# Attention on one core: scores in plain rotation of three banks, maxima handled two by two

## The reference

```
x = x + 0.5 * ffn(layernorm(x))
x = x + attention(layernorm(x), w_q, w_k, w_v, w_o)
x = x + 0.5 * ffn(layernorm(x))

attention: q, k, v = projections, split in 16 heads
           probs = softmax(q k^T / sqrt(32)),  out = (probs v) w_o^T
ffn:       relu((x sign(up)^T) * up_scale) sign(down)^T * down_scale * output_scale
```

## Time and profile before

| | |
|---|---|
| median of three runs | 3001.04 us (2997.48 to 3006.79) |
| profiled execution | 3000.77 us |
| its span, first to last instruction | 2999.0 us |
| mean granted clock of TensorE in it | 0.993 of full speed |
| TensorE matmuls busy | 2918.1 us (97%) |
| VectorE busy | 2051.5 us (68%) |
| ScalarE busy | 1610.4 us (54%) |
| GpSimd busy | 1381.3 us (46%) |

### The profile page before, as it was taken

How to read it: one execution, slowest core, us unless ns; L and a number is a source line. 1 busy time by engine, 2 the same in 40 slices (tenths; PEclk the granted TensorE clock), 3 DMA queues, 4 the chain that set the end, 5 groups by cost and what they waited for, 6 DMA issues and landing times.

```text
span 2999.0 us, 38468 instructions
## 1 busy us (share of the span) xinstructions
PE 2918.1 (97%) x14528; PEld 1936.4 (65%) x14528; DVE 2051.5 (68%) x3050; ACT 1610.4 (54%) x2851; POOL 1381.3 (46%) x522
## 2 busy tenths in 40 slices
PE   6999998998999999999999999999999999999999
PEld 5888887887755555555555555555555448888887
DVE  5555555777778787878787878787878355555553
ACT  5444444332266666666666666666666554333333
POOL 0000000000089898988898888888888730000000
PEclk9999999999999999999999999999999989999999
DMA  4110112554398989898989898989898872222100
GB/s 154 57 57 28 29 30 79 189 195 167 131 221 188 228 197 227 198 230 194 225 199 228 198 229 195 224 200 225 199 228 197 225 209 71 56 57 57 57 29 29
DMA packets 189274, 459.97 MB, mean 153 GB/s; under 512 B 90272, under 2 KB 91296, under 8 KB 148768
## 3 DMA queue, kind: packets, MB, share of 16 engines
q0 software_dynamic: 36720, 267.40, 39.0%
q1 hardware_dynamic: 152368, 190.11, 22.2%
HBM read 121.91 MB, written 67.63 MB: 63 GB/s over the span
## 4 chain that ended last, share of the span: by engine, by line
PE 85%; ACT 8%; DVE 3%; DMA 1%; issue 1%; POOL 0%; ACTq 0%; SPq 0%; DVEq 0%; POOLq 0%
PE bank L951 16%; PE bank L511 15%; PE bank L530 15%; PE bank L920 15%; PE bank L924 11%; PE bank L642 7%; ACT att_p L908 7%; PE bank L382 3%; PE bank L975 1%; PE bank L967 1%; DMA att_dma_acc<-att_p 1%; DVE norm_inv L109 1%; ACT head_raw L286 0%; DVE norm_work L119 0%; PE bank L176 0%
## 5 line engine op out<-in xcount | busy, mean ns | idle before, releaser
L853 DVE TENSOR_REDUCE att_row_max<-bank 128x1 f32<-128x512 f32 x2048 | 1255.4, 682 | 343.7 <-PE bank L924 343.7
L908 ACT ACTIVATE att_p<-bank 128x512 f32<-128x512 f32 x2048 | 1042.3, 624 | 437.6 <-PE bank L920 431.3
L809 POOL TENSOR_TENSOR att_acc<-att_acc,att_p 128x2048 f32<-128x2048 f32 x217 | 1049.6, 4837 | 46.1 <-ACT att_p L908 41.4
L920 PE MATMUL bank<-att_q,att_k 98*128 98x512 f32 x2048 | 856.3, 420 | 25.9 <-ACT att_p L908 17.8
L924 PE MATMUL bank<-att_k,att_q 96*128 96x512 f32 x2048 | 808.8, 397 | 10.8 <-DVE att_row_max L853 10.3
L920 PEld LDWEIGHTS bank<-att_q,att_k 98*128 98x128 f32 x2048 | 385.8, 189 | 424.1 <-issue 209.1
L951 PE MATMUL bank<-att_p,att_v 128*32 128x512 f32 x4096 | 501.2, 607 | 0.0
L443 DVE TENSOR_TENSOR ffn_hid_lo<-ffn_hid,ffn_hid_hi 128x512 fp32r<-128x512 f32 x256 | 175.9, 688 | 418.5 <-ACT ffn_hid_hi L486 399.7
L483 ACT ACTIVATE ffn_hid<-bank,up_s 128x512 f32<-128x512 f32 x256 | 176.0, 688 | 483.8 <-PE bank L511 482.4
L924 PEld LDWEIGHTS bank<-att_k,att_q 96*128 96x128 f32 x2048 | 389.8, 190 | 62.3 <-DVE att_row_max L853 13.1
L511 PE MATMUL bank<-hi,ffn_up_w 128*128 128x512 f32 x1024 | 400.2, 391 | 10.7 <-DVE lo L123 10.7
(11 more groups left out here) (104 smaller groups left out, 2235.9 us busy)
## 6 DMA issues: line engine op xcount, KB each, us to landing
att_dma_acc<-att_p POOLq DMA_DIRECT2D x225, 1024.0 KB, 8.9
att_dma_acc<-att_dma_acc POOLq DMA_DIRECT2D x30, 1024.0 KB, 12.4
x<-x_after_ffn SPq DMA_DIRECT2D x16, 1024.0 KB, 7.4
att_q<-q_hi SPq DMA_DIRECT2D x64, 256.0 KB, 4.1
att_k<-k_hi SPq DMA_DIRECT2D x64, 256.0 KB, 10.6
x_after_ffn<-x_out SPq DMA_DIRECT2D x8, 1024.0 KB, 9.4
q_hi<-qkv_o_hi SPq DMA_DIRECT2D x32, 256.0 KB, 2.0
q_lo<-qkv_o_lo SPq DMA_DIRECT2D x32, 256.0 KB, 2.3
```

The costliest lines, as they stand in the source:

```text
L809: self.nc.gpsimd.tensor_tensor(self.acc[H % 2][:], a[:], self.prob[kt % PR][:], ALU.add).then_inc(self.summed, 1)
L853: self.nc.vector.tensor_reduce(self.row_max[odd][:, qt, q:q + 1], m[:], axis=AX.X, op=ALU.max).then_inc(self.m_read, 1)
L908: self.nc.scalar.activation(self.prob[kt % PR][:, q * CH:(q + 1) * CH], self.s_ps[S_BANK[kt * QC + q]][:], ACT.Exp, scale=SCALE).then_inc( ...
L920: self.nc.tensor.matmul(self.s_ps[S_BANK[i]][:], self.k_st[H % NB][0:KM, kt * P:(kt + 1) * P], self.q_st[H % NB][0:KM, q * CH:(q + 1) * CH ...
```

## The change

The scores take the three banks in plain rotation, counted through all heads (unit i of all 2048 takes bank i mod 3), and always wait for the exponential three units before. `bank_order` goes.

For the maxima of the heads' groups, TensorE waits only before the even one of two, for the banks of both: that is the wait that the odd one had before. (Where one of the two slots was used by the sums or the transpose, it waits for both in turn.) And only the odd one signals, adding two to `m_ready`. VectorE waits before either reduction of a pair for that signal. It still adds one to `m_read` after each. The first maxima, among the projections, stay as they were. The number and shape of all matmuls, reductions and exponentials is the same.

```diff
-def bank_order(units, banks, second):
...
-S_BANK, S_FREED = bank_order(UNITS, SR, (23, 46))
...
-    def reduce_block(self, dve, N, m, odd, qt, q):
-        dve.wait_ge(self.m_ready, N + 1)
+    def reduce_block(self, dve, N, m, odd, qt, q, ready=1):
+        dve.wait_ge(self.m_ready, N + ready)
...
-                self.reduce_block(dve, UNITS * (H + 1) + AHEAD + p, self.m_ps[m_bank(H, slot(p))], T % 2, (kt + LEAD) % KT, q)
+                self.reduce_block(dve, UNITS * (H + 1) + AHEAD + p, self.m_ps[m_bank(H, slot(p))], T % 2, (kt + LEAD) % KT, q, 2 - q % 2)
...
-            self.nc.scalar.activation(self.prob[kt % PR][:, q * CH:(q + 1) * CH], self.s_ps[S_BANK[kt * QC + q]][:], ACT.Exp,
+            self.nc.scalar.activation(self.prob[kt % PR][:, q * CH:(q + 1) * CH], self.s_ps[(UNITS * H + kt * QC + q) % SR][:], ACT.Exp,
                                       scale=SCALE).then_inc(self.exp_done, 1)
...
     def scores(self, pe, H, kt, q):
-        i = kt * QC + q
-        if UNITS * H + S_FREED[i] > 0:
-            pe.wait_ge(self.exp_done, UNITS * H + S_FREED[i])
-        self.nc.tensor.matmul(self.s_ps[S_BANK[i]][:], self.k_st[H % NB][0:KM, kt * P:(kt + 1) * P],
+        i = UNITS * H + kt * QC + q
+        if i >= SR:
+            pe.wait_ge(self.exp_done, i - SR + 1)
+        self.nc.tensor.matmul(self.s_ps[i % SR][:], self.k_st[H % NB][0:KM, kt * P:(kt + 1) * P],
                               self.q_st[H % NB][0:KM, q * CH:(q + 1) * CH], start=True, stop=True).then_inc(self.s_ready, 1)
 
-    def maxima(self, m, T, qt, q):
-        self.nc.tensor.matmul(m[:], self.q_st[T % NB][0:KQ, qt * P:(qt + 1) * P], self.k_st[T % NB][0:KQ, q * CH:(q + 1) * CH],
-                              start=True, stop=True).then_inc(self.m_ready, 1)
+    def maxima(self, m, T, qt, q, ready=1):
+        ins = self.nc.tensor.matmul(m[:], self.q_st[T % NB][0:KQ, qt * P:(qt + 1) * P], self.k_st[T % NB][0:KQ, q * CH:(q + 1) * CH],
+                                    start=True, stop=True)
+        if ready:
+            ins.then_inc(self.m_ready, ready)
...
                     at = slot(QC * kt + q)
-                    self.bank_free(pe, H, at)
-                    self.maxima(self.m_ps[m_bank(H, at)], T, (kt + LEAD) % KT, q)
+
+                    if q % 2 == 0:
+                        if not {at - MR, at + 1 - MR}.isdisjoint((SUMS_SLOT, TURN_SLOT)):
+                            self.bank_free(pe, H, at)
+                        self.bank_free(pe, H, at + 1)
+                    self.maxima(self.m_ps[m_bank(H, at)], T, (kt + LEAD) % KT, q, 2 * (q % 2))
```

## The result

The changed kernel takes 3135.65 us (median of four runs, 3132.56 to 3138.79) against 3001.81 us for the one before (four runs). The ratio is 1.0445, with a 95% interval of 1.0427 to 1.0462: 4.5% slower, where 4.6% (3139 us) was forecast. The profiled execution of the changed kernel is the longest of its four (3138.79 us, span 3137.0); its span is 138.0 us above the 2999.0 of the kernel before.

What follows compares the result with a forecast made beforehand. TensorE, busy 97% of the span, was taken to set the pace; 8 x 0.73 + 0.13 - 1.38 = +4.59 us a regular head, +138 over all heads on 3000.77 gave 3139 us, range 3110 to 3160.

Steps and rivals of the forecast that it cites:

- the group of 5.80 us: Clean distance between output blocks in a head before the change; other groups' stalls beyond it total 1.38 us a head.
- The sum: All heads: a regular head +4.59 us, heads 2 to 29 128.5, with heads 0, 1, 30 and 31 +138 in all.
- The rotation alone: Score stalls ending groups 2 and 5 vanish: 0.86 us a head, 26 us over 30 heads, without the pairing.
- reduction 0 at 1.23, m4 at 2.57, m6 at 3.77: Times after a group's first score: first reduction, fifth and seventh maxima start later, so each group grows by 0.73 us.
- The negation in group 6: VectorE's negation between the first two reductions of group 6 is no longer covered by slack: +0.13 us a head.
- Head 1: TensorE's wait for exps, behind ScalarE's output weight copy, swallows about one group's growth: +3.9 us.
- Head 30: ScalarE's wait for GpSimd's scaling hides the rest of the growth: +1.0 us for the head.
- Head 0: No head behind it, so smaller stalls to absorb: +5.0 us.
- Head 31: Last head, no maxima, TensorE waits for exps anyhow: 0 change.
- The clock: Rival: gaps on TensorE bring 1.2 GHz, a group costs about 4 us more; 3240 us or more, 4%.
- rule of an increment's cost: About 26 ns per matmul increment; 984 fewer would be worth an estimated 26 us. The forecast took nothing.
- one wait instead of two: Rival: the fifth maximum's delay spares the seventh its wait; a group loses 0.46 us, about 3073 us, 8%.

Runs made afterwards that it cites:

- the halves: Two kernels, each with plain rotation: only the odd maximum signals, adding two (3045.93 us); or TensorE waits for both banks before the even one, each maximum signalling (3028.04 us).
- the shorter reductions: Two kernels: the changed kernel with VectorE reducing only 384 (3019.84 us) or 256 (2972.85 us) of 512 columns in the heads, exponents scaled down.
- the last kernel above: Plain rotation, maxima one by one, ScalarE's output copy moved before the group's first exp, and the transpose issued between its group's two output tiles: 2971.60 us, ratio 0.9881.
- the kernel with 384 columns: The changed kernel with VectorE reducing only 384 of 512 columns of each bank in the heads, exponents scaled down: 3019.84 us, ratio 1.0044.
- 256 columns: The changed kernel with VectorE reducing only 256 of 512 columns of each bank in the heads, exponents scaled down: 2972.85 us, ratio 0.9887.
- the kernel with paired signals: Plain rotation, TensorE waits for each bank by itself as before, but only the odd maximum signals, adding two: 3045.93 us, ratio 1.0144.
- paired waits alone: Plain rotation, every maximum signals by itself, but TensorE waits before the even one for both banks: 3028.04 us, ratio 1.0086.

## Why the prediction was right, point by point

- **TensorE sets the pace; the group of 5.80 us is the unit.** Right. All of a regular head's difference is made of groups.
- **The sum.** The mechanism was right, but that the sum is this close is in part luck. Of the 138.0 us between the two profiled executions, heads 2 to 29 give 123 (forecast 128.5), head 0 gives 4.7 (5.0), head 1 2.1 (3.9), head 30 2.1 (1.0), and head 31 with all behind it 5.2 (0); the last 0.6 lies before the heads. A term 5 us too large and one of 5 us put at nothing cancel. By the medians the change is +134 us.
- **The rotation alone is worth 26 us, and nothing beside the pairing.** Right: 24 us less by the medians (3003.12 of its own comparison to 2979.07), and 54.2 us a regular head with either rotation once the pairs are in.
- **The pairing: reduction 0 at 1.23, m4 at 2.57, m6 at 3.77, 0.73 a group.** Right to 0.01 at each step, and shown by the halves and by the shorter reductions to be this mechanism.
- **The negation in group 6: +0.13.** The record has 6.77 there. The forecast's parts give 6.53 + 0.13 + 0.28 = 6.94. The transpose was taken over at 0.28; but in the kernel before it had itself waited for a reduction, which in the changed kernel is done by its turn. Its weight load in the kernel before, then load and matmul in the changed one:

```profile
1458.46 0.09 PEld L943 LDWEIGHTS bank<-ident,att_neg_max 128*16 128x16 f32 x1 [0.41 <-DVE att_row_max L853]
```

```profile
1513.16 0.09 PEld L928 LDWEIGHTS bank<-ident,att_neg_max 128*16 128x16 f32 x1
...
1513.37 0.27 PE L928 MATMUL bank<-ident,att_neg_max 128*16 128x128 f32 x1
```

  The load is now done before the matmul's turn. This is the one term of a regular head that was off, by 0.17: +4.4 a head and not +4.59, so 5 us of the sum.
- **Head 1: +3.9.** It took 55.3 us, so +2.1: its long stall is in group 4, which took 9.21 us before and 7.62 after, against 5.89 and 6.55 in head 12. The stall shrank from 3.3 to 1.1 us and so swallowed the growth of three groups, where one was forecast. **Head 30: +1.0**, the record has +2.1. **Head 0: +5.0**, the record has +4.7.
- **Head 31: 0.** The head itself got shorter (60.8 instead of 68.2 us from its first score to its last output matmul, by the timelines), and what follows longer: 570.7 instead of 558.2 us ('s stretch ends where that begins). Together +5, from 626.4 to 631.7 us counted from head 31's first score. The chain of waits has there

```profile
2537.40 15.15 DMA prob_sums<-head_total
```

  a small transfer of sums, with VectorE's reciprocal and the second feed-forward's norm behind it. That isn't shown to be the reason: the chain has the same transfer at 14.82 us with the rotation alone, whose end takes 626.9. Over the other kernels here the end varies from 626.9 to 632.6 us, and not with the pairing: 627.8 with the pairs alone, 630.6 in the last kernel above, which has no pairs. So the 5 us can't be put down to the change; the cause stays open. It is 4% of the difference.
- **The rivals.** The clock stayed at 1.00 in a regular head, though TensorE waits twice a group. The Trainium skill's rule of an increment's cost ("TensorE: Matmul & The Clock Gate", The cost: per-tile semaphore tail) isn't borne out here: m0 to m3 start 1.41 us apart for six steps (1487.67 to 1489.08), so 0.235, with half of the maxima's signals and waits gone. That is the figure of before; not even the 0.008 came. The chance of one wait instead of two had its picture in the kernel with 384 columns, where only m4 waited and a group lost 0.24.

## What to carry to other kernels

Look at a loop between two engines in time, not in shares: VectorE was idle a fifth of each head, and had 0.3 us of slack in the only place where it counted (0.12 for the weight load). Grouping signals starts the consumer later, grouping waits asks for its result earlier, and with four banks in twos that is double buffering of pairs: here the two delays met on one loop and cost more than their sum (0.73 a group against 0.32 and 0.26). It isn't enough that the consumer keeps the producer's pace of one block in 0.47 us (0.235 x 2): with 384 columns the reductions did (0 to 3 start 0.47 apart), and a group still lost 0.24. With 256 columns the second reduction of a pair ended (2.01) before the next pair's turn (2.22), and nothing was lost. A stall that is removed gives its time back only if no other stall of the same group already covers it, so a small gain (the rotation) has to be measured without the big loss beside it.

## What the runs showed of the hardware

- A matmul's increment of two reached VectorE as soon as an increment of one: reduction 0 starts 0.44 us after m1 (1488.13 to 1488.57), as it started 0.43 after m0 before. Half of the maxima's increments and waits changed nothing in the distance of TensorE's matmuls, 0.235 us.
- A wait that stands before a matmul holds its weight load too: m4's load and m4 itself both start at 1489.91 in the changed kernel, just after reduction 1 ends. A bank that came free after the load's turn and before the matmul's cost 0.06 to 0.11 us in the kernel with paired signals. After a full stall the next matmul came 0.33 to 0.34 after the released one instead of 0.235 (705.14 to 705.48 in the kernel before, 1489.91 to 1490.25 in the changed one, 1445.93 to 1446.26 with paired waits alone, 1446.87 to 1447.20 with 384 columns).
